# Row maxima in seven tiles of 128 mixed query columns, one transpose per head group, and new places for every unit

## The reference

```python
qh = proj(q, Wq, bq); kh = proj(k, Wk, bk); vh = proj(v, Wv, bv)       # 16 heads of 32
scores = jnp.einsum('bhqd,bhkd->bhqk', qh, kh) / math.sqrt(D_K)
attn = jax.nn.softmax(scores, axis=-1)
out = jnp.einsum('bhqk,bhkd->bhqd', attn, vh)
x = x + out.transpose(0, 2, 1, 3).reshape(B, -1, D_MODEL) @ Wo.T + bo
x = x + ffn(_layernorm(x))          # fp4_linear for gate, up and down
```

## Time and profile before

| | |
|---|---|
| median of the runs | 2343.65 us |
| the profiled execution | 2341.8 us, span 2339.8 us |
| PE busy | 2206.3 us, 94% |
| DVE busy | 1802.4 us, 77% |
| ACT busy | 845.3 us, 36% |
| POOL busy | 199.9 us, 9% |

### The profile page before, as it was taken

How to read it: one execution, slowest core, us unless ns; L and a number is a source line. 1 busy time by engine, 2 the same in 40 slices (tenths; PEclk the granted TensorE clock), 3 DMA queues, 4 the chain that set the end, 5 groups by cost and what they waited for, 6 DMA issues and landing times. The chain is left out here.

```text
span 2339.8 us, 50409 instructions
## 1 busy us (share of the span) xinstructions
PE 2206.3 (94%) x17444; PEld 1866.8 (80%) x17444; DVE 1802.4 (77%) x3107; ACT 845.3 (36%) x1677; POOL 199.9 (9%) x226
## 2 busy tenths in 40 slices
PE   5999999999999999999999999975999999999998
PEld 4888788887888888888888788853788888888886
DVE  5767777777677776777767777747999999999986
ACT  4544444454444444444445444433111111111111
POOL 1110111110101101111110110100000000000000
PEclk9999999999999999999999999987999999999999
DMA  5343434434344344343443434325010100100100
GB/s 161 100 119 87 120 84 118 121 81 125 94 108 123 80 124 111 91 116 88 114 121 90 120 85 119 88 75 159 17 38 27 38 29 27 40 27 27 36 18 27
DMA packets 124001, 197.38 MB, mean 84 GB/s; under 512 B 29776, under 2 KB 72272, under 8 KB 121280
## 3 DMA queue, kind: packets, MB, share of 16 engines
q1 hardware_dynamic: 123840, 194.86, 30.0%
HBM read 75.67 MB, written 23.33 MB: 42 GB/s over the span
## 5 line engine op out<-in xcount | busy, mean ns | idle before, releaser
L611 DVE TENSOR_REDUCE row_max<-max_bank 112x1 f32<-112x376 f32 (+1 forms) x1024 | 523.0, 541 | 347.8 <-PE max_bank L470 342.8
L536 ACT ACTIVATE probs<-score_bank 125x448 f32<-125x448 f32 x768 | 404.7, 543 | 319.5 <-PE score_bank L485 311.7
L470 PE MATMUL max_bank<-k_high,q_masked 128*112 128x376 f32 (+1 forms) x1024 | 313.0, 353 | 17.1 <-DVE row_max L611 12.8
L485 PE MATMUL score_bank<-qstack,kstack 100*128 100x224 f32 x1536 | 301.7, 281 | 27.6 <-issue 23.7
L485 PEld LDWEIGHTS score_bank<-qstack,kstack 100*128 100x128 f32 x1536 | 262.6, 190 | 59.6 <-issue 51.6
L1145 ACT ACTIVATE f_act_gate<-gate_bank 128x512 f32<-128x512 f32 (+1 forms) x84 | 47.3, 563 | 516.4 <-PE up_bank L1100 516.4
L500 PE MATMUL pv_bank<-probs,values 125*32 125x224 f32 x3072 | 225.1, 366 | 9.2 <-ACT probs L536 9.2
L1100 PE MATMUL gate_bank<-ffn_gate_hi,f_xqt 128*128 128x512 f32 (+1 forms) x672 | 218.9, 387 | 8.1 <-DVE f_xqt L1206 8.1
L444 PE MATMUL proj_bank<-wv_hi,ctx_hi 128*128 128x256 f32 x768 | 221.2, 288 | 4.3 <-DVE wo_lo L690 4.3
L506 PE MATMUL pv_bank<-probs,ones 125*32 125x224 f32 x3072 | 219.4, 358 | 0.0
L444 PE MATMUL proj_bank<-wv_hi,ctx_lo 128*128 128x256 f32 x768 | 216.6, 282 | 0.0
(11 more groups left out here) (121 smaller groups left out, 4166.1 us busy)
## 6 DMA issues: line engine op xcount, KB each, us to landing
kstack<-k_high SPq DMA_DIRECT2D x512, 93.8 KB, 2.2
ctx_raw<-in_ctx SPq DMA_DIRECT2D x16, 1500.0 KB, 6.9
kstack<-k_low SPq DMA_DIRECT2D x256, 93.8 KB, 2.2
qstack<-q_part SPq DMA_DIRECT2D x768, 28.0 KB, 1.9
ffn_quant<-fw_share SPq DMA_DIRECT2D x48, 176.0 KB, 1.9
fw_raw<-ffn_quant SPq DMA_DIRECT2D x33, 256.0 KB, 4.1
xn<-in_x SPq DMA_DIRECT2D x16, 448.0 KB, 7.9
res<-in_x SPq DMA_DIRECT2D x16, 448.0 KB, 4.0
```

Of the source, the lines that this page charges most:

```text
L470: nc.tensor.matmul(out[0:QH, 0:hi - lo], q_masked[t % 2][:, j, half * QH:(half + 1) * QH], k_part[t % 2][0][:, lo:hi], start=True, stop=Tr ...
L485: last = nc.tensor.matmul(score_bank[j % 2][:, k * SQ:(k + 1) * SQ], kstack[t % 2][0:STK, j, kt * KW:kt * KW + P], qstack[t % 2][:, j, :], ...
L536: nc.scalar.activation(probs[p][:, j, :, :], score_bank[j % 2][0:KW, 0:2 * SQ].rearrange("p (k q) -> p k q", k=2), ACT.Exp, scale=float(DK ...
L611: nc.vector.tensor_reduce(row_max[:, half, j, kh:kh + 1], mbank[0:QH, 0:KSPLIT[kh + 1] - KSPLIT[kh]], AX.X, ALU.max).then_inc(max_reduced, 1)
```

## The change

The four heads' masked query columns are taken as one row of 896, which is cut into seven tiles of 128 columns; a tile can hold columns of two heads. The maximum matmuls become 14 of 128 columns, with 14 reductions over 128 partitions. One transpose of all 7 x 128 negated maxima follows. `qstack` gets seven extra rows in place of four: row m holds the maxima of tile m in its own 128 columns and zero elsewhere, and DVE writes all seven with one product of the transposed bank and the identity. `kstack`'s seven rows are ones. The copies on ACT go. A projection of values of the first half waits explicitly for the low part of the context, and the reciprocal waits for the low part of the group before. All units have new places, in one table for each slot; the three *pv* units can stand anywhere up to place 14, which means up to 2 in the next slot.

```diff
-STK = SHIFT + HG
+MT = HG * SQ // P
+STK = SHIFT + MT
...
+def attend_units(g):
+    at = PLACES[g % NG]
+    return [(place, (kind, g, p)) for kind, places in (("pv", "pv"),) for p, place in enumerate(at[places])]
...
+    placed += [(place, unit) for place, unit in attend_units(g) if place < 12]
+    if not (first and g == 0):
+        placed += [(place - 12, unit) for place, unit in attend_units(g - 1) if place >= 12]
...
-        "shift": (5.97, 10.64),
-        "pv": (6.66, 11.9),
-        "pv_last": 0.15,
+        "shift": 9.78,
+        "pv": (10.65, 13.42, 13.42),
...
                 elif kind == "v":
                     half, kt = u[2], u[3]
+                    if half == 0 and kt == 0:
+                        reached(pe, lo_done["ctx"], count(b, "ctx", t, KC - 1))
...
-                    nc.tensor.matmul(out[0:QH, 0:hi - lo], q_masked[t % 2][:, j, half * QH:(half + 1) * QH],
+                    nc.tensor.matmul(out[:, 0:hi - lo], masked_columns[t % 2][:, m * P:(m + 1) * P],
                                      k_part[t % 2][0][:, lo:hi], start=True, stop=True).then_inc(made["max"], 1)
...
-                    nc.tensor.transpose(out[:, 0:QH], neg_max[:, u[2], :],
-                                        ident[0:QH, 0:QH]).then_inc(made["shift"], 1)
+                    nc.tensor.transpose(out[:, 0:P], neg_max[:, :], ident[:, :]).then_inc(made["shift"], 1)
...
-                elif kind == "shift":
-                    act.wait_ge(made["shift"], count(b, *u))
-                    row = mbank[SHIFT:STK, 0:QH].unsqueeze(1).to_broadcast([HG, HG, QH])
-                    nc.scalar.activation(qstack[t % 2][SHIFT:STK, :, u[2] * QH:(u[2] + 1) * QH], row,
-                                         ACT.Copy).then_inc(shift_copied, 1)
...
+                elif kind == "shift":
+                    dve.wait_ge(made["shift"], count(b, *u))
+                    reached(dve, made["score"], count(b, "score", t - 2, 2, 3))
+                    nc.vector.tensor_tensor(shift_rows[t % 2][SHIFT:STK, :, :],
+                                            mbank[SHIFT:STK, 0:P].unsqueeze(1).to_broadcast([MT, MT, P]),
+                                            ident[SHIFT:STK, SHIFT:STK].unsqueeze(2).to_broadcast([MT, MT, P]),
+                                            ALU.mult).then_inc(shift_copied, 1)
...
+                    reached(dve, lo_done["sum"], count(b, "sum", t - 1))
                     reached(dve, made["pv"], count(b, "pv", t, 2))
```

More of the change, by code:

```diff
@@ L55 @@
 FFN_SLOTS = (0, 1, 3)
[L58 to L66, removed]
@@ L91 @@
         "load": 2.6,
         "load_res": 6.6,
-        "ffn_quant": (3.25, 4.97, 6.08, 6.45, 7.12, 8.21, 8.35, 9.18, 9.62, 10.0, 10.54),
-        "ffn_store": 11.6,
-    },
-    {
[L97 to L116, removed]
+        "add_bias": 11.9,
@@ L117 @@
         "load": 2.6,
         "load_res": 6.6,
-        "ffn_quant": (3.81, 4.25, 4.6, 4.7, 5.64, 7.25, 8.05, 8.99, 9.45, 11.45, 11.51),
-        "ffn_store": 11.6,
-    },
-    {
[L123 to L142, removed]
+        "add_bias": 11.9,
@@ L143 @@
         "load": 2.6,
         "load_res": 6.6,
-        "ffn_quant": (3.62, 3.73, 3.88, 4.04, 5.72, 8.89, 9.04, 9.14, 9.78, 10.37, 11.36),
-        "ffn_store": 11.6,
-    },
-    {
[L149 to L168, removed]
+        "add_bias": 11.9,
@@ new lines @@
+        "ffn_quant": (3.82, 3.85, 4.85, 5.64, 6.06, 6.16, 6.17, 7.48, 10.37, 10.79, 11.9),
+        "ffn_store": 11.9,
+    },
+    {
+        "max": (0.05, 0.14, 0.74, 0.83, 1.02, 1.47, 4.34, 4.67, 4.84, 5.72, 6.4, 6.92, 7.56, 8.71),
+        "shift": 11.39,
+        "pv": (8.41, 11.95, 13.09),
+        "inverse": (0.71, 1.71),
+        "heads": 4.23,
+        "heads_hi": 7.89,
+        "sum_lo": 11.04,
+        "k": (0.87, 4.69),
+        "k_lo": (2.1, 4.87),
+        "q": 6.32,
+        "q_lo": 7.65,
+        "v": (2.49, 6.45, 10.36),
+        "out": (2.97, 11.9),
+        "ctx": (0.5, 0.51, 2.63, 5.2),
+        "xt": (5.48, 5.71),
+        "xt_lo": (0.05, 6.03),
+        "norm": (10.81, 11.9),
+        "norm2": (0.05, 4.23),
@@ L244, in start_units @@
     units += [("stack_low", 0), ("stack", 0), ("split_w", 2)]
-    m = [("max", 0, n) for n in range(16)]
+    m = [("max", 0, n) for n in range(2 * MT)]
     v = [("v", 0, 0, n) for n in range(KT)]
@@ L359, in index_of @@
             return ((b + unit[1]) * 2 + unit[2]) * KT + unit[3]
-        per = {"score": 12, "max": 16, "shift": 2, "k": 2, "q": 1, "pv": 3, "sum": 1}
+        per = {"score": 12, "max": 2 * MT, "shift": 1, "k": 2, "q": 1, "pv": 3, "sum": 1}
         if kind in per:
```

134 lines of the change are left out of this document (88 added, 46 removed).

## The result

The changed kernel takes 2400.26 us (median of 4 runs, 2392.57 to 2404.39), the kernel before, beside it, 2347.42 (2338.21 to 2354.36): a ratio of 1.0234, 95% interval 1.0208 to 1.026. It is slower by 2.3%; the forecast had said 2312 us, 1.3% faster. The profiled execution took 2396.14 us around a span of 2394.3, 84 above the forecast for it.

What follows compares the result with a forecast made beforehand. PE's own list of matmuls was taken to set the time. Per batch -2.7 of PE work, -1.5 of old stalls and +2.35 of new ones gave -1.85 us; times 16, -30 from 2341.8: 2312 us, range 2284 to 2340.

Steps and rivals of the forecast that it cites:

- The jump: End of slot 3: the loop's jump back, counted as 1.92 us in that slot.
- Instructions taken from PE: Eight maximum matmuls and four transposes fewer, value products in 9 runs instead of 12: 2.7 us of PE less per batch.
- The 128-column load: Maximum matmuls load 128 columns instead of 112: charged nothing, taken as hidden; 0.7 us per batch if each showed.
- The product on VectorE: DVE's new products of 7 x 896 elements, four per batch: 1.09 us each, bounds 0.93 to 1.68.
- The three named stalls: Old PE waits for a third maximum, exponentials and a slot 0 transpose: 1.5 us per batch to be won.
- Slot 2 into 3: First score of slot 3 waits for DVE's product: new stall of 1.25 us per batch, between 1.1 and 1.85.
- Score four of slot 1: In slot 1 it comes 0.6 us after score two, before its exponential: stall of 0.3 to 0.4 us.
- SP's stacking in slot 0: Stacking DMAs start 0.8 us into slot 0, so slot 1 waits: stall 0.7 us, between 0 and 3.
- Slot 3 into 0: At the loop's end a value product and the jump cover the wait for DVE's product, done at 5.3 us: no stall.
- B: Rival: half clock after the 1.25 us gap into slot 3 gives the gain back, 2339 us, no change; chance 0.12.
- C: Rival: SP becomes the bound, as stacks wait for a late quantization chain; slot 0 lasts 23.1 us, 2368 us; chance 0.13.
- the 12% for slower: Chance of 0.12 that the changed kernel measures slower, resting mostly on C.

Runs made afterwards that it cites:

- both heads at slot 0: TensorE's loop head placed on the first slot of a 16 KB code block: changed kernel 2331.85 us, kernel before 2346.95 us.
- the hint: Prefetch hint for TensorE's jump back, at the top of each loop pass: changed kernel 2293.33 us (its head in its own place), kernel before 2306.71 us.

## Why the prediction was wrong

The forecast's terms for the new order come out within a microsecond a batch, but that is half of its 1.85. What failed above all is a step that the prediction passed over in half a sentence, "1.92 in slot 3 for the loop's jump", taken as a constant of the loop. What follows the jump depends on where TensorE's code lies, and the changed kernel's head lay badly; that the changed number of instructions ahead of the loop and in it put it there is likely, but no run shows it. Counted by the medians, the change was to bring -30 us and brought +53. By its steps:

- **The jump.** Late code behind the first score, with the half clock after it: 2400.26 to 2331.85, 68 us. This alone turns the forecast's sign; shown from both sides, by taking it from the changed kernel and giving it to the kernel before. With both heads at slot 0 the change brings -15 us (2346.95 to 2331.85), so 68 of the 83 us are this step. The other 15 stand at the jump too: its own wait is 2.84 us a pass there instead of 1.78, 14 us in 13 passes, and half clock follows in 9 passes instead of 7.
- **Why that wait is longer.** In all eight kernels here that jump without the hint, the packet that lands last ahead of the first score starts 2.9 to 3.1 us ahead of it on average. In the kernels that end a pass with a value projection PE still works for 1.2 us of this, in those that end it with value products for 0.2. So the new order covers 1 us less of the same fetch. What sets off the fetch, and why it comes so late behind the 32 short matmuls of a value product, is open: no run changed the last unit alone.
- **Instructions taken from PE**, 2.7 us a batch: with the hint on both sides PE's busy time falls from 91.10 to 89.05, 2.05, by overlapping records. Right in kind, 0.65 short. The 128-column load, charged with nothing, is not quite hidden: the starts of two adjacent maxima lie 186 ns apart (median, with the hint) instead of 173, those of a maximum and a score 175 instead of 172. The Trainium skill (TensorE: Matmul & The Clock Gate, LDWEIGHTS) would charge 13 ns each, an estimate from that page; the trace agrees where two maxima are adjacent.
- **The product on VectorE**, taken as 1.09 us: 1.10 (64 times, mean 1097 ns). Right.
- **The three named stalls**, 1.5 us to be won: with the hint they cost the kernel before 1.35 a pass, and the changed one nothing. Right.
- **Slot 2 into 3**, a stall of 1.25: PE idle for 1.26. Right. **Score four of slot 1**, 0.3 to 0.4: 0.24 a pass, 0.4 at most. Near.
- **SP's stacking in slot 0**, 0.7: not there. Slot 0 lasts 19.18 with the hint, below the 19.6. It is close, though: the last transfer lands 0.33 us ahead of slot 1's first score, and once the product's waits are covered that score waits for it.
- **Slot 3 into 0**: no stall foretold, since "a value product and the jump" were to cover the product. In the changed kernel they do: the product ends 2.2 us ahead of the first score on average. (Its terms for VectorE add up to 5.5 us, not the 5.3 that it states; the trace has 5.6 on average.) But the cover is the jump alone. With the hint the product costs 0.99 us a batch, since VectorE runs five quantizing steps and the heads' low half between the negation and the product, as shown below. So about 1 us a pass is missing from the forecast at this place either way, as the longer wait of the jump or as the wait for the product. With the jump gone, -1.85 + 0.99 for the product + 0.65 for the instructions - 0.7 for the stacking gives -0.91, and -0.94 was measured: two of the misses cancel, which is luck.

```profile
732.64 0.17 DVE L609 TENSOR_REDUCE neg_max<-row_max 128x7 f32<-128x14 f32 x1
732.74 0.34 DVE L847 TENSOR_SCALAR fw_power<-fw_power 128x352 f32<-128x352 f32 x1
...
735.06 0.45 DVE L661 SCALAR_TENSOR_TENSOR o_part<-heads,biases,o_part 128x224 fp32r<-128x224 f32 x1
735.54 1.10 DVE L615 TENSOR_TENSOR qstack<-max_bank,ident 7x896 fp32r<-7x896 f32 x1
```

- **The rivals.** B had the right tool, idle PE and then half clock, at the wrong place: slot 3 has clock 1.00 behind its 1.26 us gap. C had the right sign and came nearest (2368) by a cause that did not occur: SP's stacks were waited for 3 times, 7.0 us in all. None named the code, so the 12% for slower stood for something else.

## What to carry to other kernels

Where a wait is put down to "issue" at a loop's jump, look at the packets of the instruction queue, and treat the wait as a property of where the code lies and of what the engine still has to do when the fetch starts: an edit can move both, so fix the loop head or give the jump its hint before judging a change of a few per cent. Compare an edit with both sides in that state; here it turned +2.3% into −0.6%. And a wait hidden behind another is not gone: covering the product's waits gave 4 us with the slow jump in place, and 20 to 25 once it was gone (with somewhat different places).

## What the runs showed of the hardware

- A 16 KB packet of code took 0.9 to 2.2 us around the jump of the changed kernel, and the first score came 1.9 us after the last one had landed. One that PE needed at once behind the jump stopped it for 1.8 to 5.6 us, and half clock (0.50) followed in 25 of 26 passes: 39 us in the kernel before, 68 in the changed one.
- With the hint, the whole run has 29 code packets in both kernels, instead of 146 (159 in the changed kernel with its own head): 9 packets a pass ((146 - 29) / 13) no longer appear. Worth 40 us, 1.7%, to the kernel before by one parameter. Written out, without any jump, the changed kernel fetched 117 packets, waited for none, and was no faster (2292.95 against 2293.33).
- A VectorE step on 128x352 took 1.48 to 1.50 us instead of 0.53 each of the 16 times that it ran beside POOL's addition of 112x512 (the run with the residual in mid-slot).
